# Output projection as three f16 products, with its bias added to the residual rows by accumulating DMAs

## The reference, cut to what matters

```python
def xattn(x, latents, mask, ...):          # x is the context, latents the normed rows
    xn, ln = layernorm(x, ln_x_g, ln_x_b), layernorm(latents, ln_l_g, ln_l_b)
    q = ln @ W_q
    kv = jnp.concatenate([xn @ W_kv, ln @ W_kv], axis=1)
    ...                                     # heads, rmsnorm of q and k, softmax over all keys
    out = jnp.einsum('bhij,bhjd->bhid', attn, v)
    return out.transpose(0, 2, 1, 3).reshape(b, nl, INNER) @ W_out + b_out

x = x + xattn(ctx_1024, _layernorm(x), mask, ...)
x = x + ffn(_layernorm(x), w1, conv_w, conv_b, w2)   # act_quant, w1, conv of 3 taps, silu, act_quant, w2
```

## Time and profile before

| | |
|---|---|
| Time, median of 3 runs | 439.9 us (439.56 to 439.93) |
| Span of the profiled execution | 436.6 us |
| Outside the span (439.9 less 436.6) | 3.3 us |
| PE busy | 406.0 us, 93% |
| DVE busy | 377.0 us, 86% |
| ACT busy | 313.9 us, 72% |
| POOL busy | 86.1 us, 20% |

### The profile page before, as it was taken

The page is one execution under the profiler, slowest core; times in us unless marked ns, Lnnn a source line. Parts: engine busy times, 40 slices in busy tenths (PEclk is TensorE's granted clock), DMA queues, the critical chain, the costliest instruction groups (busy, mean ns, idle before and its releaser), DMA issues.

```text
span 436.6 us, 13819 instructions
## 1 busy us (share of the span) xinstructions
PE 406.0 (93%) x5914; PEld 275.4 (63%) x5914; DVE 377.0 (86%) x598; ACT 313.9 (72%) x367; POOL 86.1 (20%) x115
## 2 busy tenths in 40 slices
PE   1999997799999999999999999999999988899985
PEld 1666675566666666666666666666676644576664
DVE  4789987987887889789879879889879899999994
ACT  2456767589979756757666766767666589999984
POOL 2175554850000120020120020111001010221200
PEclk9999999999999999999999999999999998999999
DMA  7802000612111111111211111111101000001002
GB/s 215 226 2 72 2 2 1 227 44 74 50 40 63 38 39 62 51 38 47 67 38 39 62 39 51 62 39 41 49 33 44 3 0 0 2 26 48 26 26 80
DMA packets 27588, 22.53 MB, mean 52 GB/s; under 512 B 7232, under 2 KB 27268, under 8 KB 27524
## 3 DMA queue, kind: packets, MB, share of 16 engines
q1 hardware_dynamic: 26112, 21.59, 15.2%
q10 hardware_dynamic: 1412, 0.01, 0.2%
HBM read 6.91 MB, written 2.10 MB: 21 GB/s over the span
## 4 chain that ended last, share of the span: by engine, by line
PE 56%; DVE 25%; ACT 12%; issue 3%; DMA 2%; ACTq 0%; DVEq 0%; POOL 0%
PE sc L1691 14%; DVE arena L722 14%; PE heads L1708 7%; PE heads L1709 5%; PE heads L1710 5%; PE heads L1517 4%; ACT arena L1290 3%; PE sc L1528 3%; ACT qq L1379 3%; PE by L1596 2%; ACT qq L1387 2%; PE bx L1528 2%; PE by L1528 2%; PE sc L1795 2%; DMA lng<-in_L_xattn_ln_x_b 2%
## 5 line engine op out<-in xcount | busy, mean ns | idle before, releaser
L722 DVE SCALAR_TENSOR_TENSOR arena<-arena 128x1024 bf16<-128x1024 f32 x160 | 194.0, 1243 | 30.2 <-ACT arena L1290 29.1
L1290 ACT ACTIVATE arena<-sc,kb 128x1024 f32<-128x1024 f32 x160 | 169.9, 1115 | 67.6 <-PE sc L1691 67.5
L1708 PEld LDWEIGHTS heads<-v,arena 128*128 128x128 bf16 x1280 | 117.1, 97 | 39.2 <-issue 28.3
L1708 PE MATMUL heads<-v,arena 128*128 128x65 f16 x1280 | 130.2, 194 | 3.8 <-DVE arena L722 3.5
L1709 PE MATMUL heads<-v,arena 128*128 128x64 f16 x1280 | 129.3, 195 | 0.0
L1710 PE MATMUL heads<-v,arena 128*128 128x65 f16 x1280 | 128.7, 192 | 0.0
L1691 PE MATMUL sc<-qs,kst 64*128 64x512 f16 x960 | 118.0, 378 | 2.2 <-DVE kk L664 1.5
L1709 PEld LDWEIGHTS heads<-v,arena 128*128 128x128 bf16 x1280 | 118.8, 97 | 0.1
L1710 PEld LDWEIGHTS heads<-v,arena 128*128 128x128 bf16 x1280 | 118.8, 99 | 0.0
L1691 PEld LDWEIGHTS sc<-qs,kst 64*128 64x128 f16 x960 | 40.0, 94 | 48.1 <-issue 5.0
L519 POOL TENSOR_SCALAR frs<-fmv 128x2 f32<-128x2 f32 x8 | 7.9, 990 | 150.9 <-DVE fmv L790 150.9
(11 more groups left out here) (215 smaller groups left out, 586.4 us busy)
## 6 DMA issues: line engine op xcount, KB each, us to landing
kst<-kk SPq DMA_DIRECT2D x80, 128.0 KB, 2.0
xs<-in_x SPq DMA_DIRECT2D x8, 256.0 KB, 5.4
qs<-qq SPq DMA_DIRECT2D x16, 128.0 KB, 2.0
out<-cbuf SPq DMA_DIRECT2D x7, 256.0 KB, 2.1
xs<-in_ctx SPq DMA_DIRECT2D x6, 256.0 KB, 5.3
xs<-in_L_ffn_w SPq DMA_DIRECT2D x1, 1024.0 KB, 6.8
cbuf<-in_L_ffn_w SPq DMA_DIRECT2D x1, 1024.0 KB, 8.8
arena<-in_L_xattn_W_kv SPq DMA_DIRECT2D x2, 256.0 KB, 5.0
```

The lines of the kernel that those rows point to most:

```text
L722: e.scalar_tensor_tensor(out=rest[:, j, :, :], in0=prob[:, j, :, :], scalar=SHRINK, in1=probh[:, j, :, :], op0=ALU.mult, op1=ALU.subtract) ...
L1290: a_.activation(prob[:, j, :, :], sc[(j + 1) % 2][:, :, :], ACT.Exp, bias=kb[:, bass.ds(i * QUAD + j, 1)]).then_inc(exp_done[j], 1)
L1708: t_.matmul(o, hi, row[:, 0:OW], start=first and sub == 0, stop=False, skip_group_check=True)
```

## The change

The attention output and W_out (scaled by 64) are each split into a high and a low f16 part, and the projection is the sum of high by high, high by low and low by high. POOL makes both splits. The bias is no longer put into PSUM by PE: eight DMAs from POOL's queue, with addition, put it onto the rows `xs` once the projections of q, k and v have read them. DVE multiplies the bank by 1/64 in the instruction that adds it. The last two pairs of row tiles keep their f32 product, without the bias matmul.

```diff
@@ SP's loads @@
-                sp.dma_start(bout[:, 0, :], b_out.rearrange("(a d) -> a d", a=1).to_broadcast([3, D])).then_inc(s["w_rest"], 16)
@@ POOL @@
-            def copy_heads(b):
+            def split_heads(b):
                 wait(pool, "ot_ps", b)
-                g.tensor_copy(ost, att[:, bass.ds(b * 2, 2), :]).then_inc(s["ost_ready"], 1)
+                pair = att[:, bass.ds(b * 2, 2), :]
+                g.tensor_copy(ost16[:, 0, :, :], pair).then_inc(s["ost_high"], 1)
+                pool.wait_ge(s["ost_high"], b + 1)
+                pool.sem_inc(s["passed"], 1)
+                g.tensor_tensor(ost16[:, 1, :, :], pair, ost16[:, 0, :, :], ALU.subtract).then_inc(s["ost_ready"], 1)
-            def split_bias():
...
+            def bias_to_rows():
+                pool.wait_ge(s["z_ready"], XP)
+                pool.sem_inc(s["passed"], 1)
+                row = b_out.rearrange("(a t d) -> a t d", a=1, t=1)
+                for n in range(XP):
+                    pool.dma_start(xs[:, 2 * n:2 * n + 2, :], row.to_broadcast([P, 2, D]), accum_op=ALU.add).then_inc(s["bias_in"], 16)
+
+            def split_wout():
+                pool.wait_ge(s["w_rest"], 48)
+                step = Chain(pool, s["wout_step"], 0)
+                scaled = wout_scaled[:, :, :]
+                step(g.tensor_scalar(scaled, wout[:, :, :], WOUT_SCALE, None, ALU.mult))
+                step(g.tensor_copy(wout16[:, 0, :, :], scaled))
+                g.tensor_tensor(wout16[:, 1, :, :], scaled, wout16[:, 0, :, :], ALU.subtract).then_inc(s["wout_ready"], 1)
+
+            bias_to_rows()
+            split_wout()
@@ DVE @@
-            def add_attention(b):
+            def add_attention(b, scale=1.0 / WOUT_SCALE):
                 dve.wait_ge(s["y_ps"], b + 1)
-                e.tensor_tensor(pair_of_tiles(b), rows_bank(b)[1].rearrange("p (t d) -> p t d", t=2), pair_of_tiles(b), ALU.add).then_inc(s["x1_ready"], 1)
+                e.scalar_tensor_tensor(out=pair_of_tiles(b), in0=rows_bank(b)[1].rearrange("p (t d) -> p t d", t=2), scalar=scale, in1=pair_of_tiles(b),
+                                       op0=ALU.mult, op1=ALU.add).then_inc(s["x1_ready"], 1)
...
+                dve.wait_ge(s["bias_in"], 16 * XP)
@@ ACT @@
-                a_.activation(ot.rearrange("p t k c -> p (t k c)"), rows_bank(b)[0], ACT.Copy).then_inc(s["ot_ready"], 1)
+                a_.activation(ot16.rearrange("p w t k c -> p (w t k c)"), rows_bank(b)[0].bitcast(F16), ACT.Copy).then_inc(s["ot_ready"], 1)
@@ PE @@
-                for t in range(2):
-                    for k in range(KD):
-                        last = t_.transpose(rows_bank(b)[0][:, (t * KD + k) * P:(t * KD + k + 1) * P], ost[:, t, k * P:(k + 1) * P], ident[:, :])
+                for w in range(2):
+                    for t in range(2):
+                        for k in range(KD):
+                            at_ = ((w * 2 + t) * KD + k) * P
+                            last = t_.transpose(rows_bank(b)[0].bitcast(F16)[:, at_:at_ + P], ost16[:, w, t, k * P:(k + 1) * P], ident16[:, :])
-            def bias_first(b):
-                t_.matmul(rows_bank(b)[1], one16[0:3, :], bparts[:, 2:4, :].rearrange("p a d -> p (a d)"), start=True, stop=False, skip_group_check=True)
             def out_project(b):
                 pe.wait_ge(s["ot_ready"], b + 1)
-                for t in range(2):
+                wait(pe, "x1_ready", b)
+                for t in range(2):
+                    n = 0
                     for k in range(KD):
-                        last = t_.matmul(rows_bank(b)[1][:, t * D:(t + 1) * D], ot[:, t, k, :], wout[:, k, :], start=False, stop=(t == 1 and k == KD - 1), skip_group_check=True)
+                        for h_, w_ in ((0, 0), (0, 1), (1, 0)):
+                            last = t_.matmul(rows_bank(b)[1][:, t * D:(t + 1) * D], ot16[:, h_, t, k, :], wout16[:, w_, k, :], start=(n == 0), stop=(n == 5))
+                            n += 1
@@ PE, the last two pairs: late_heads_first, late_project @@
-                bias_first(b)
-                        last = t_.matmul(..., ot_late[i][:, t, k, :], wout[:, k, :], start=False, ...)
+                        last = t_.matmul(..., ot_late[i][:, t, k, :], wout[:, k, :], start=(k == 0), stop=(k == KD - 1))
```

More of the change, by code:

```diff
@@ L38 @@
 SHRINK = 1.0 - 0.75 / 256.0
+WOUT_SCALE = 64.0
 class Chain:
@@ L137, in xattn_ffn @@
         ones = sb("ones", [P, P], F32)
-        bout = sb("bout", [3, 2, D], F32)
-        bparts = sb("bparts", [3, 4, D], F16)
+        wout16 = sb("wout16", [P, 2, KD, D], F16)
         lng = sb("lng", [P, 2, KD, 2], F32)
@@ L142, in xattn_ffn @@
         gq = sb("gq", [P, 4], F32)
+        wout_scaled = sb("wout_scaled", [P, KD, D], F32)
         cw = sb("cw", [P, J, 3], F32)
@@ L195, in xattn_ffn @@
         ost = cbuf[:, 0:2 * D].rearrange("p (t d) -> p t d", t=2)
+        ost16 = cbuf[:, 0:2 * D].bitcast(F16).rearrange("p (w t d) -> p w t d", w=2, t=2)
         ot = cbuf[:, 2 * D:4 * D].rearrange("p (t k c) -> p t k c", t=2, k=KD)
+        ot16 = cbuf[:, 2 * D:4 * D].bitcast(F16).rearrange("p (w t k c) -> p w t k c", w=2, t=2, k=KD)
         probf = prob[:, :, :, :].rearrange("p k e c -> p (k e c)")
@@ L231, in xattn_ffn @@
             wmean_ready wround_ready wq_ready wt_ps wt_ready out_ready rec_step
-            heads_done ost_ready ot_ps ot_ready y_ps bias_step bias_ready x1_ready prep_step rstd2_step
+            heads_done ost_high ost_ready ot_ps ot_ready y_ps wout_step wout_ready bias_in x1_ready prep_step rstd2_step
             rstd2_ready dq_ready xd_ps xd_ready h_ps edge_ps center_ready left_ready taps_done edge_step edge_done
@@ L559, in _ @@
                         pool.wait_ge(s["heads_done"], c * HP + HP)
-                    copy_heads(b)
+                    split_heads(b)
                     prep_scale(b)
@@ L736, in weights_mean @@
                 e.reciprocal(wmean[:, 2:4], wmean[:, 0:2]).then_inc(s["wmean_ready"], 2)
-                dve.wait_ge(s["w_rest"], 64)
+                dve.wait_ge(s["w_rest"], 48)
                 e.tensor_scalar(cw[:, :, :], cw[:, :, :], wmean[:, 0:1], None, ALU.mult)
@@ L1006, in feed_forward @@
                 right_tap(0, 3)
-                add_attention(NB - 2)
+                add_attention(NB - 2, 1.0)
                 edge_taps(0, 0)
@@ L1012, in feed_forward @@
                 left_tap(0, 4)
-                add_attention(NB - 1)
+                add_attention(NB - 1, 1.0)
                 row_stats(NB - 1, 2)
@@ L1711, in values, with quad @@
                     return mm
-                def quad(c, hp, unit, n, i, first, nxt, shifted, between=None, ahead=None):
+                def quad(c, hp, unit, n, i, first, nxt, shifted, between=None):
                     score(c, hp, n, 2, shifted)
                     score(c, hp, n, 3, shifted)
-                    if ahead is not None:
-                        wait(pe, "x1_ready", ahead)
-                        bias_first(ahead)
                     if first:
@@ L1766, in attention @@
                             weights_total()
-                    pe.wait_ge(s["bias_ready"], 1)
+                    pe.wait_ge(s["wout_ready"], 1)
                     def unit(cc, hp, nxt):
@@ L1773, in unit @@
                         base = nq * (b + HP)
-                        quad(c, hp, b + HP, base, 0, True, None, shifted, ahead=b)
+                        quad(c, hp, b + HP, base, 0, True, None, shifted)
                         pe.wait_ge(s["wt_ready"], 4)
@@ L1868, in late_project @@
                     for k in range(KD):
-                        last = t_.matmul(rows_bank(b)[1][:, t * D:(t + 1) * D], ot_late[i][:, t, k, :], wout[:, k, :], start=False, stop=(t == 1 and k == KD - 1), skip_group_check=True)
+                        last = t_.matmul(rows_bank(b)[1][:, t * D:(t + 1) * D], ot_late[i][:, t, k, :], wout[:, k, :], start=(k == 0), stop=(k == KD - 1))
                 last.then_inc(s["y_ps"], 1)
```

## The result

The changed kernel takes 453.7 us, median of 4 runs (452.75 to 455.24); beside it the kernel before took 439.9 us (439.56 to 440.33). The ratio is 1.032, 95% interval 1.029 to 1.035. The forecast was 444.3 us in a range of 438.0 to 449.0: the sign came true, the size didn't, +13.8 us instead of +4.4.

The account below looks back on a forecast made before the run. Bound by PE (56% of the chain), DVE (25%) and ACT (12%) taking turns. From 439.9 us: -3.1 arithmetic, +3.6 splits, +4.0 late keys, -0.1 last pairs, giving 444.3 us; range 438.0 to 449.0.

Parts of the forecast that it names:

- part 3: Bias transfers from 79.88 us: they delay the key refill PE reads at 89.41 us, +4.0 us.
- Half of them, as two queues that take turns would have it: Key refill near 89 us: four of eight transfers served first, 4 x 1.1 = 4.4 us, less 0.4 margin.
- C: Rival, full price: all eight transfers first, 8.4 us of wait, 1.0 us in unit middles; 450.2 us, chance 0.10.
- just here the queue is full and the margin is 0.4 us: Near 80 to 89 us: argument against the rival that keys are not late (440.0 us, chance 0.27).
- Part 1, PE's arithmetic: Projection in each unit: f16 products and transposes save 0.52 us a unit, -3.1 us over six.
- Gain: 0: Unit start: dropping the 0.31 us bias matmul saves nothing, since PE waits for DVE's second remainder anyway.
- Part 2, POOL's splits: Units b = 0, 2, 4: POOL's subtraction holds DVE remainders, +2.1 us at starts and +1.5 us in middles.
- The start: Start of units b = 0, 2, 4: fourth remainder held 1.0 us, PE waits 0.7 us; +2.1 us.
- The middle: Middle of units b = 0, 2, 4: 0.65 us of subtraction beside L796, 0.5 holds the next remainder; +1.5 us.
- 3 x 1.0: Upper bound for the subtraction's hold in the middle of units b = 0, 2, 4; lower bound 0.
- Part 4: Last pairs, 349 to 351 us: two bias matmuls of 0.3 us go; -0.1 us, bounds -0.6 and +0.1.
- `split_bias`: Near 84 us: its removal gains an estimated 0.6 us, hidden by the wait for keys; 0 with it, -0.6 without.

Follow-up runs that it names:

- experiment 5: Changed kernel with the eight bias transfers as plain copies, without the addition (residual rows lost): 458.3 us, ratio 1.042.
- experiment 6: Changed kernel with the eight accumulating transfers reading rows of x instead of the one bias row: 443.8 us, ratio 1.009.
- experiment 7: Changed kernel with the bias row first laid into every SBUF partition by one load, the additions reading it there; W_out scaled in place: 444.0 us, ratio 1.009.
- experiment 3: Changed kernel with the eight transfers issued later, after the sums of w1 and w2 and the split of W_out: 451.8 us, ratio 1.026.
- experiment 4: Changed kernel with sixteen transfers of 128 KB, each issued behind another exponential, instead of eight of 256 KB: 440.4 us, ratio 1.0023.
- experiment 9: Kernel before without split_bias and its bias matmul (bias in no output): 439.1 us, ratio 0.9993.
- Experiment 8: Changed kernel without the bias transfers and DVE's wait for them, POOL's subtraction on 256 instead of 512 elements: 436.7 us, ratio 0.993.
- experiment 1: Changed kernel without the eight bias transfers and DVE's wait for them (bias in no output): 440.2 us, ratio 1.0015.
- experiment 2: Kernel before with the eight accumulating transfers in place of split_bias and the bias matmuls: 450.7 us, ratio 1.025.

## Why the prediction was right in sign and wrong in size

**The step that failed** is a term of part 3: "What one costs: w1 and w2, 2 MB, are done within 8.8 us, 1.1 us for 256 KB". It measured 3.3 us. That price was taken from loads whose packets read distinct rows. The only doubt I priced was an addition that "moved its bytes twice" (2.2 us each, left outside the range); the source I didn't look at. Experiments 5, 6 and 7 show that it is the source. With another one the same eight transfers cost 3.5 us at the first division (experiment 6), against the +4.0 of the forecast; that agreement is partly luck, because a packet of these transfers is even then slower than one of the hardware queue (97 against 41 ns), while POOL issues only one transfer each 1.25 us:

```profile
80.16 10.04 POOL L551 DMA_DIRECT2D xs<-in_L_xattn_b_out  x8
```

The second error of the same step is its shape. "Half of them, as two queues that take turns would have it" gives one wait; in truth the engines were full until about 113 us, so PE waited three times, and ran at the low clock after two of the waits, for which the forecast had no term. No rival had a higher price than 1.1 us; C, with all of it at 450.2, was nearest. The Trainium skill's "DMA: Bandwidth & Descriptors", section "Issuing engines are not separate DMA queues", was borne out: the refills on SP's queue slowed to 9.7 us beside POOL's. The section goes on that the time to start a transfer is usually small beside the transfer; here POOL needed 10.04 us for eight, 1.25 each against the 3.3 that one took to move: not small, but less than their own pace.

**Where the transfers stood** ("just here the queue is full and the margin is 0.4 us") mattered less than forecast: experiment 3 moved them 26 us later for 451.8 instead of 453.7 us. It mattered that many were in flight together: experiment 4.

**Part 1, PE's arithmetic**: "0.52 us a unit". Units with b = 1, 3, 5 went from 33.64 to 33.11 us, -0.53. Right. The chain of waits in unit b = 0:

```profile
163.30 0.45 PE bx L1599 x8
163.75 1.40 PE sc L1705 x12
...
166.73 1.31 PE by L1609 x12
168.04 1.40 PE sc L1705 x12
...
172.96 1.62 DVE arena L731
174.58 1.49 DVE arena L806 x2
176.07 1.13 DVE arena L731
```

Twelve products take 1.31 us in the chain, the old eight 1.81. "Gain: 0" for the bias matmul was right (experiment 9). The addition kept its time: 0.68 us against 0.69.

**Part 2, POOL's splits**: "+2.1" and "+1.5", 1.2 us for each unit with b = 0, 2, 4. These units grew by 1.00 us though the arithmetic saved 0.52: the splits cost 1.5 us each, 4.6 in all against 3.6. *The start* was right. Two remainders of b = 0, ns min/median/max:

```profile
L731 DVE SCALAR_TENSOR_TENSOR arena<-arena x2: 1631/1902/2172, 158.6 to 160.2; 128x1024 bf16<-128x1024 f32 x2
```

The fourth takes 2172 ns, 0.95 us more than the 1217 ns of the earlier trace rows, and in PE's timeline the first value matmul behind it waits:

```profile
162.39 0.20 PE L1722 MATMUL heads<-v,arena 128*128 128x65 f16 x1 [0.49 <-DVE arena L731]
```

from 161.71 to 162.39, 0.68 us instead of the usual step of 0.03: 0.65, where 0.7 was forecast. *The middle* cost 0.84 instead of 0.5. "L796, which reads one tile and may run beside it" was wrong: the same instruction, now L806, was held. DVE's timeline, then POOL's:

```profile
174.51 1.56 DVE L806 TENSOR_SCALAR arena<-xs,fmv,frs 128x256 f32<-128x256 f32 x2
175.99 1.21 DVE L731 SCALAR_TENSOR_TENSOR arena<-arena 128x1024 bf16<-128x1024 f32 x1
```
```profile
172.90 0.60 POOL L518 CAST cbuf<-xs 128x512 f16 x1
173.69 1.91 POOL L521 TENSOR_TENSOR cbuf<-xs,cbuf 128x512 f16<-128x512 f16 x1 [0.19 <-POOL cbuf L518]
```

POOL's subtraction is issued at 173.69, waits for the remainder to end near 174.5, and ends at 175.60; the first of the two L806 takes 1240 ns, the second 400, and the remainder that I thought would pay is not held at all (1.21). The bound of "3 x 1.0" held it. (The forecast works with 1.25 us for the subtraction at one place and 1.15 at the other; undisturbed, at 92.56 us, POOL takes 1.15.) The forecast had cited the page "SBUF — State Buffer", section "Who interferes with whom", of the Trainium skill for instructions with a single SBUF input; the same section excepts modes that take the shared port pair, and names TENSOR_SCALAR among the operations that can enter one, which I left out. The 1240 ns agree with that; that the instruction runs in such a mode, no row shows. Experiment 8 ties the cost to the subtraction's length: half of it gives back 0.97 of the 1.5 us.

**Part 4 and `split_bias`**: nothing of "-0.1" can be told from the spread. That what `split_bias` costs is covered by the keys was right: in experiment 9, without it, PE is ready for them 0.9 us before they land instead of 0.4 us after, and the first division comes only 0.2 us earlier. By these two executions its cost was nearer 1.3 us than 0.6.

**The last stage**, +2.2 us in this execution, I don't put down to the change: with the same instructions there it took 437.3 - 348.2 = 89.1 us in experiment 1's execution, 0.6 less than before, 89.7 in experiment 3 and 90.6 in experiment 4. What differs is the clock. Tables of windows at the same point of the work, the changed kernel, then the kernel before 14 us earlier:

```profile
376.00:390.00 14.00, 11.92 (x89) 7.47 (x90) 12.42 (x26) 10.65 (x16) 1.20 (x4) 0.63 0.01 2
```
```profile
362.00:376.00 14.00, 11.45 (x100) 6.79 (x100) 13.89 (x28) 13.31 (x19) 1.93 (x6) 0.88 0.01 2
```

A mean granted clock of 0.63 against 0.88. Why it stays low for longer in one execution than in another isn't shown. The traces differ by 12.7 + 1.5 + 2.2 = 16.4 us, the medians by 13.8. The changed kernel's median is 1.5 us under its profiled execution. And the 3.3 us around the span of before are too many: wherever time and span of that kernel stand on record together, they are 2.1 to 2.25 apart, so its profiled execution took about 438.8 us, 1.1 under the median. These 2.6 us are the difference; the forecast's base, the median, isn't touched by it.

**What stays open.** A plain copy from distinct rows through POOL's queue wasn't run, so how much of the 97 ns is the addition and how much the queue can't be said. That one row in the chip's memory is slow to read when many packets ask for it at once is shown by the pace (187 ns here, 104 with the transfers spread out); what in the memory limits it isn't.

## What to carry to other kernels

Price a transfer by its source pattern as well as its bytes: a broadcast that reads one small row thousands of times is to be laid into SBUF once (13.8 us of loss became 3.9), or spread out (nothing was left of it), and what pays for it is whoever waits for small refills on the same engines. Ask first what there is to gain: the bias matmul that these transfers replaced cost nothing (experiment 9). Ask how long the DMA engines stay full, not when the first waiter is late: each refill in that time is late again, and PE's clock may fall with each wait. When f16 parts are to be made of something that PE transposes anyway, make them from PSUM behind the transpose: POOL's subtraction of 1.15 us in SBUF held DVE instructions beside it by 0.84 and 0.95 us.

## What the runs showed of the hardware that was not expected

- 2048 packets of 1 KB that all read one row of HBM, in eight transfers at once: 187 ns a packet in the changed kernel, 256 KB in 3.3 us with all 16 engines full (79 GB/s), and 0.049 x 448.9 x 16 / 2176 = 162 ns in experiment 2. The same packets from distinct rows or from SBUF: 97 ns. Plain copies of that row go in 640 packets, 512 of them of 4 KB (0.045 x 456.5 x 16 / 640 = 514 ns on the mean), with 20.5 us of the engines in all against 22.0 to 25.4, and one refill of keys beside them took 23.7 us.
- POOL takes 1.25 us to issue an accumulating transfer of 256 KB (10.04 us for eight), whatever its source.
- A POOL subtraction of 128x512 takes 1.15 us undisturbed and held a DVE remainder by 0.95 us and a TENSOR_SCALAR of 0.40 us with a single tensor operand by 0.84.
- After waits of up to 4.8 us PE ran its next group of scores at 0.50 to 0.54 of full clock, and at 1.00 the one after the third wait.
